# Layer 0's edge sum of a two-layer graph network: runs of equal nodes added up on VectorE ahead of the matmul

## The chip, the cores and the metric

The kernel runs on one core of a Trainium2 chip. The metric is the device time of one execution, in microseconds (us). Engines are named as the profile does: PE is TensorE (PEld its weight loads), DVE VectorE, ACT ScalarE, POOL GpSimd, SP SyncE. A q behind the name is the engine's own sequencer.

## The reference

12,500 nodes with 128 features, 200,000 edges sorted by their destination `dst`, 50 features per edge.

```python
h = relu(layernorm(x))
x = x + (segment_sum(h[src], dst) @ W_rel.T + b_rel + h @ W_root.T)      # layer 0
h = relu(layernorm(x))
edge_weights = silu(edge_attr @ We1 + be1) @ We2 + be2                   # layer 1
agg = segment_sum(h[src] * edge_weights, dst)
x = x + (silu(agg @ Wn1 + bn1) @ Wn2 + bn2)
```

Everything is float32.

## The kernel before

The edges are cut into tiles of 128, four tiles to a block of 512 (`BLOCK`), 391 blocks, and 17 blocks (`U`) to one of 23 iterations (`ITERS`). Three blocks are a group (`GB`): six groups per iteration (`G`), five of 12 tiles and a last one of 8. Since the edges are sorted, those of a group lie within a window of 128 neighbouring nodes, whose first node is `sum_base`.

GpSimd gathers the rows of h by `src`, one indirect DMA per tile, 68 per iteration (L324), into `rows`, which holds one whole iteration. Before it gathers a group it waits (`hold`, L192) for the sum of the same group of the iteration before, `s_seg`; at the first and the fourth group it also waits for the indices, which SyncE loads half an iteration at a time.

For each group VectorE compares an iota with the tiles' `dst` less the window's base and gets a one-hot of 128 x 1536 (L744, `s_onehot`). TensorE multiplies the rows of each of the 12 tiles with its one-hot and accumulates in the bank `seg` or `ew_a` in turn (L377, `s_seg`): the transposed sum of the window. One group later VectorE reads the window's base into a register and adds the bank to `agg` at that place (`add_window`, L752 to L756). `agg` lies as 128 features x 12,800 nodes.

In the same iterations one group of 512 nodes is finished per iteration (`node_update0`): ScalarE copies `agg` and h, TensorE multiplies (L388, L389, at group 1), VectorE adds bias and x and takes the statistics for layer 1's layer norm (group 3), the shift (group 4) and y (group 5).

Before all this there are a setup (windows of all groups, from the block minima and maxima of `dst`) and the h phase, five passes over five groups of 512 nodes each, in which h is computed and written to `h_rows`. GpSimd gathers iteration 0 meanwhile, from x, since h isn't there; iteration 0 therefore applies the layer norm to the gathered rows itself, block by block (L658 to L669). The whole of layer 0 may run over several passes, if a window is wider than 128 nodes; the number is computed on the chip (`plan`), and is one here.

Layer 1 runs in 23 iterations of the same shape, with the edge network of each block and the same one-hots and sums.

Each engine has its own queue of instructions in the order in which it is written out; semaphores alone tie them together. In particular nothing but `s_onehot`, the landed rows and, for GpSimd, `s_seg` orders the three engines in layer 0.

## Time and profile before

| what | us |
|---|---|
| median of 3 runs | 4755.86 (4752.82 to 4757.91) |
| the profiled execution | 4776.76 |
| its span | 4774.7 |
| setup and h phase, to 162 | 162 |
| iteration 0, 162 to 248 | 86 |
| layer 0, 248 to 2293, 21 periods | 2045 |
| end of layer 0, 2293 to 2391 | 98 |
| layer 1, from 2391 | 2383 |

The stages are cut by the timeline, at the first one-hot of VectorE, at its first add of iteration 1, and at the starts of the later iterations. A row of the timeline gives the start, the busy time, the engine, the line and the operation, and in brackets the time for which the engine was idle before it and what ended that. "issue" means that it waited for nothing that the profile shows, "remote" a semaphore whose sender isn't told.

### The profile page before, as it was taken

How to read it: one execution, taken by the hardware profiler on the slowest of the kernel's cores; microseconds unless marked ns; L12 is line 12 of the kernel's file. 1: busy time of each engine (PE TensorE's matmuls, PEld its weight loads, DVE VectorE, ACT ScalarE, POOL GpSimd, SP SyncE). 2: the span in 40 equal slices, each digit the busy share in tenths (PEclk: the TensorE clock that was granted, in tenths of full speed). 3: DMA queues.
4: the chain of work that ended last, by engine and by line, in shares of the span. 5: the costliest groups of instructions: out<-in, count | busy, mean ns of one | idle time of the engine just before them, and what ended most of it. 6: DMA issues, size and time to landing. Idle time of an engine off the chain costs nothing.

```text
span 4774.7 us, 34714 instructions
## 1 busy us (share of the span) xinstructions
PE 2496.3 (52%) x10150; PEld 1646.9 (34%) x10150; DVE 1005.3 (21%) x1790; ACT 704.4 (15%) x1212; POOL 2967.1 (62%) x3135
## 2 busy tenths in 40 slices
PE   1332322323232322233347777777776777777778
PEld 0232322222232322232224444444443444434444
DVE  2511111111111111111312222222222222222223
ACT  2400000000000000000112222222222222212222
POOL 5366666666666666666466666666666666666663
PEclk9765655555555655655668777877777877877878
DMA  4212222212222222212212222222222222222222
GB/s 131 67 52 54 52 55 56 54 51 56 54 56 54 53 54 55 54 51 56 64 53 70 65 63 65 68 65 70 66 66 62 69 65 70 66 63 68 66 65 62
DMA packets 230577, 296.69 MB, mean 62 GB/s; under 512 B 68707, under 2 KB 160277, under 8 KB 230432
## 3 DMA queue, kind: packets, MB, share of 16 engines
q0 software_dynamic: 100096, 205.20, 16.6%
q10 hardware_dynamic: 61378, 60.59, 4.6%
q1 hardware_dynamic: 69086, 30.73, 2.4%
q8 instruction: 5, 0.08, 0.0%
q14 instruction: 12, 0.10, 0.0%
HBM read 269.81 MB, written 26.48 MB: 62 GB/s over the span
## 4 chain that ended last, share of the span: by engine, by line
another core or an unknown queue 44%; PE 28%; issue 17%; DVE 6%; DVEq 2%; ACT 1%; POOL 0%; DMA 0%; ACTq 0%; SPq 0%; POOLq 0%
PE seg L377 10%; PE hid_b L419 3%; PE hid_a L424 3%; DVE onehot L744 3%; PE ew_a L377 2%; PE hid_c L424 2%; PE ew_b L430 2%; PE hid_b L424 2%; PE ew_a L430 1%; DVEq L752 1%; PE hid_a L419 1%; PE hid_c L419 1%; DVE agg L756 1%; DVE e_stats L658 1%
## 5 line engine op out<-in xcount | busy, mean ns | idle before, releaser
L324 POOL DMA_INDIRECT rows<-h_rows,idx x3060 | 2902.0, 948 | 1723.0 <-issue 946.8
L377 PE MATMUL seg<-onehot,rows 128*128 128x128 f32 x4784 | 884.3, 340 | 1347.0 <-DVE onehot L744 523.8
L377 PEld LDWEIGHTS seg<-onehot,rows 128*128 128x128 f32 x4784 | 802.1, 250 | 1460.5 <-issue 1038.9
L377 PE MATMUL ew_a<-onehot,rows 128*128 128x128 f32 x1472 | 289.0, 324 | 574.3 <-issue 529.2
L744 DVE TENSOR_TENSOR onehot<-iota_ps,dst_rel 128x1536 f32<-128x1536 f32 (+1 forms) x278 | 461.0, 1658 | 0.8 <-DVE dst_rel L732 0.6
L377 PEld LDWEIGHTS ew_a<-onehot,rows 128*128 128x128 f32 x1472 | 246.6, 235 | 570.5 <-issue 566.5
L852 DVE TENSOR_TENSOR rows<-ew_a,rows 128x512 f32<-128x512 f32 x207 | 142.8, 690 | 1110.6 <-remote 636.3
L756 DVE TENSOR_TENSOR agg<-seg,agg 128x128 f32 x207 | 60.4, 292 | 1179.3 <-remote 1110.5
L424 PE MATMUL hid_c<-hidden,we_sb 128*128 128x512 f32 x230 | 149.4, 735 | 161.6 <-ACT hidden L601 160.4
L852 DVE TENSOR_TENSOR rows<-ew_b,rows 128x512 f32<-128x512 f32 x184 | 126.7, 689 | 507.2 <-PE ew_b L430 173.2
L424 PE MATMUL hid_a<-hidden,we_sb 128*128 128x512 f32 x278 | 219.6, 882 | 0.0
L424 PE MATMUL hid_b<-hidden,we_sb 128*128 128x512 f32 x276 | 178.8, 734 | 37.4 <-ACT hidden L601 37.4
L756 DVE TENSOR_TENSOR agg<-ew_a,agg 128x128 f32 x69 | 19.8, 288 | 802.4 <-remote 779.0
L430 PEld LDWEIGHTS ew_a<-ident,agg 128*128 128x128 f32 x828 | 127.8, 170 | 159.4 <-issue 157.0
L601 ACT ACTIVATE hidden<-hid_a,be_col 128x512 f32<-128x512 f32 x139 | 95.6, 688 | 521.8 <-remote 401.3
L601 ACT ACTIVATE hidden<-hid_b,be_col 128x512 f32<-128x512 f32 x139 | 95.6, 687 | 474.2 <-PE hid_b L419 195.1
L601 ACT ACTIVATE hidden<-hid_c,be_col 128x512 f32<-128x512 f32 x115 | 79.1, 688 | 578.2 <-remote 419.4
L534 ACT ACTIVATE n_std<-n_mv,eps 128x4 f32<-128x4 f32 x25 | 7.4, 297 | 1022.8 <-issue 702.9
L430 PE MATMUL ew_a<-ident,agg 128*128 128x128 f32 x828 | 156.6, 323 | 2.8 <-issue 2.8
L430 PEld LDWEIGHTS ew_b<-ident,agg 128*128 128x128 f32 x736 | 107.5, 163 | 132.9 <-issue 118.4
L546 ACT ACTIVATE hT<-agg 128x512 f32 x23 | 14.5, 629 | 922.7 <-DMA y_rows<-ys 917.0
L430 PE MATMUL ew_b<-ident,agg 128*128 128x128 f32 x736 | 132.9, 311 | 0.9 <-issue 0.9
(134 smaller groups left out, 1851.1 us busy)
## 6 DMA issues: line engine op xcount, KB each, us to landing
rows<-h_rows,idx POOLq DMA_INDIRECT x3060
ef_a<-ef_blocks ACTq DMA_DIRECT2D x70, 300.0 KB
node_work<-ef_blocks ACTq DMA_DIRECT2D x47, 300.0 KB
xs<-x SPq DMA_DIRECT2D x40, 256.0 KB
ys<-y_rows SPq DMA_DIRECT2D x26, 256.0 KB
out<-xs ACTq DMA_DIRECT2D x26, 256.0 KB
y_rows<-ys ACTq DMA_DIRECT2D x25, 256.0 KB
h_rows<-node_work ACTq DMA_DIRECT2D x23, 256.0 KB
```

Of the source, the lines that this page charges most:

```text
L324: pool.indirect_dma_start(out=rows[:, u, t, :], out_offset=None, in_=table, in_offset=bass.IndirectOffsetOnAxis(ap=idx[:, j:j + 1], axis=0 ...
L377: mm = pe.matmul(seg[layer][g % 2][:, 0:P], rows[:, u, t, :], onehot[:, g % 2, k * TB + t, :], start=(k == 0 and t == 0), stop=(last and t ...
L419: pe.matmul(hid_ps[u % 3][:, :], we1_sb[:, :], ef[g % 2][:, k, :], start=True, stop=True).then_inc(s_hid, 1)
L424: pe.matmul(hid_ps[u % 3][:, :], we2_sb[:, :], hidden[:, u % 2, :], start=True, stop=True).then_inc(s_ew_t, 1)
L430: tr = pe.transpose(ew_ps[u % 2][:, t * P:(t + 1) * P], weights[:, u % 2, t * P:(t + 1) * P], ident[:, :])
L546: nc.scalar.activation(hT[r], h_table[:, bass.ds(g * BLOCK, BLOCK)], ACT.Copy)
L601: nc.scalar.activation(hidden[:, u % 2, :], hid_ps[u % 3][:, :], ACT.Silu, bias=be1_col[:, :]).then_inc(s_silu, 1)
L658: op = v.bn_stats(e_stats[:, u, t, :], src[:, t, :])
L744: return v.tensor_tensor(onehot[:, g % 2, 0:tiles, :], iota_ps[:, 0:P].unsqueeze(1).to_broadcast([P, tiles, P]), dst_rel[:, bass.ds(it * U ...
L752: base = dve.value_load(base_row[0:1, bass.ds(it * G + g, 1)], min_val=0, max_val=BASE_MAX)
L756: v.tensor_tensor(window, seg[layer][g % 2][:, 0:P], window, ALU.add).then_inc(s_acc[layer], 1)
L852: v.tensor_tensor(rows[:, u, :, :], ew, rows[:, u, :, :], ALU.mult).then_inc(s_msg, 1)
```

## The change

On the host the edges of a group are dealt out differently: partition p of a group's tiles holds 12 edges that are neighbours in the sorted order (8 in the last group), where before neighbours lay in neighbouring partitions. Within such a stretch equal nodes stand together, as runs. The kernel numbers the runs of each stretch once, in the setup (`run_of`, a scan over changes of `dst`), and the nodes they belong to (`run_dst`, `run_targets`). For each group VectorE then, for three runs r (`R`), multiplies the rows with the mask of run r (`masks`, made once per iteration) into three neighbouring PSUM banks, `wide`, and reduces over the 12 edges into 128 x 128 (`run_sums`). TensorE multiplies only these three sums with three one-hots (made for three groups at a time, `one_hots`, twice per iteration). Each multiply waits for the reduce before it, and each reduce for the multiply before it, on semaphores that VectorE itself increments, all against one counter register, `done`. The add into `agg` comes two groups later (`LAG`), with its base loaded once per iteration. GpSimd waits in layer 0 for VectorE's third multiply (`s_pick[2]`) instead of TensorE's sum. TensorE's node product stands at group 2 instead of 1. If a stretch held more than three runs, layer 0 would run in further turns (`passes0`). In the setup, all of this and the clearing of `agg` and the computing of the windows stand ahead of the h phase; before, the latter two came behind it. In layer 1 the load of the base uses fewer register instructions.

The core of the diff:

```diff
+R = 3
+LAG = 2
-                    hold(pool, s_seg[layer], i * G + (g + 1))
+                    if layer == 0:
+                        hold(pool, s_pick[R - 1], i * G + (g + 1))
+                    else:
+                        hold(pool, s_seg[1], i * G + (g + 1))
...
+            v.tensor_scalar(dst_flat, dst_flat, 1.0, None, ALU.add)
+            v.memset(scratch, 1.0).then_inc(s_setup, 1)
...
+            v.tensor_tensor_scan(run_of, scratch, run_of, 0.0, ALU.mult, ALU.add).then_inc(s_setup, 1)
...
+            v.memset(agg[0][:, :], 0.0)
...
+            v.tensor_tensor(plan[:, 0:1], plan[:, 2:3], run_wrap[0:1, :], ALU.mult).then_inc(s_plan, 1)
+            run_targets(0)
...
-            v.memset(agg[0][:, :], 0.0)
...
+            def run_sums(g):
+
+                dve.reg_add(done, done, 1)
+                tiles = len(blocks_of(g)) * TB
+                first = g * GB
+                for r in range(R):
+                    dve.wait_ge(s_sum[(r + R - 1) % R], done)
+                    v.tensor_tensor(picked[:, 0:tiles, :],
+                                    rows[:, first:first + tiles // TB, :, :].rearrange("p k t f -> p (k t) f"),
+                                    run_mask[:, r, first * TB:first * TB + tiles].unsqueeze(2)
+                                    .to_broadcast([P, tiles, P]),
+                                    ALU.mult).then_inc(s_pick[r], 1)
+                    dve.wait_ge(s_pick[r], done)
+                    v.tensor_reduce(run_sum[g % SUM_BUFS][:, r, :], picked[:, 0:tiles, :].rearrange("p e f -> p f e"),
+                                    AX.X, ALU.add).then_inc(s_sum[r], 1)
+
+            def add_runs(g, base, value):
+
+                window = agg[0][:, bass.ds(base, P)]
+                dve.wait_ge(s_seg[0], value)
+                v.tensor_tensor(window, run_seg[g % 3][:, 0:P], window, ALU.add).then_inc(s_acc[0], 1)
...
                     for g in range(G):
-                        if g > 0:
-                            add_window(0, i, it, g - 1)
-                        else:
-                            add_window(0, i - 1, it - 1, G - 1)
-                        one_hot(it + (g + 1) // G, (g + 1) % G).then_inc(s_onehot, 1)
+                        if g == 0:
+                            hold(dve, s_mask, i + 1)
+                        dve.wait_ge(s_rows[0][g], landed_full if g < G - 1 else landed_last)
+                        run_sums(g)
+                        add_runs((g + G - LAG) % G, window_at[g], done)
+                        if g == LAG - 1:
+                            one_hots(it, 1)
+                        if g == HALF_G + 1:
+                            one_hots(it + 1, 0)
                         if g in steps:
                             steps[g]()
```

What stands in VectorE's queue in an iteration of layer 0 for one group. Before, the add of the group before and the next one-hot:

```order
L752 ISA
L752 TENSOR_LOAD base_row
L752 ISA x2
L754 REGISTER_ALU
L755 REGISTER_ALU [waits s_acc_done0]
L756 ISA [waits s_seg_done0]
L756 TENSOR_TENSOR agg<-seg,agg 128x128
L744 ISA
L744 TENSOR_TENSOR onehot<-iota_ps,dst_rel 128x1536
```

Now, the group with index 2 (the sums of groups lie in turn in three places, two of them in `onehot`'s memory, one in `hidden`'s):

```order
L876 REGISTER_ALU [waits s_rows0_2]
L881 TENSOR_TENSOR wide<-rows,consts_ps 128x1536 [waits s_sum2]
L887 TENSOR_REDUCE hidden<-wide 128x128 [waits s_pick0]
L881 TENSOR_TENSOR wide<-rows,consts_ps 128x1536 [waits s_sum0]
L887 TENSOR_REDUCE hidden<-wide 128x128 [waits s_pick1]
L881 TENSOR_TENSOR wide<-rows,consts_ps 128x1536 [waits s_sum1]
L887 TENSOR_REDUCE hidden<-wide 128x128 [waits s_pick2]
L894 ISA [waits s_seg_done0]
L894 TENSOR_TENSOR agg<-seg,agg 128x128
```

One long instruction per group became six, each with a wait for the one ahead of it, and the load of the base is gone.

TensorE's queue at the same place, before, with the node product behind group 0:

```order
L399 ISA
L406 ISA [waits s_onehot]
L377 MATMUL seg<-onehot,rows 128x128 [waits s_rows0_0]
L377 MATMUL seg<-onehot,rows 128x128 x11
L385 ISA
L388 MATMUL node<-w_root_sb,hT 128x128 [waits s_nT]
L389 MATMUL node<-w_rel_sb,node_work 128x128
```

and now, groups 0 and 1 and then the node product:

```order
L406 MATMUL seg<-onehot 128x128 [waits s_sum2]
L406 MATMUL seg<-onehot 128x128 x2
L404 REGISTER_ALU
L406 MATMUL ew_a<-onehot 128x128 [waits s_sum2]
L406 MATMUL ew_a<-onehot 128x128 x2
L424 ISA
L427 MATMUL node<-w_root_sb,hT 128x128 [waits s_nT]
L428 MATMUL node<-w_rel_sb,node_work 128x128
```

Twelve matmuls became three, both of whose operands VectorE writes, and the product moved one group back.

## Rows read from the trace of the kernel before

**Rows 1.** The costliest group of instructions; busy us, mean ns, idle before it:

```profile
L324 POOL DMA_INDIRECT rows<-h_rows,idx x3060 | 2902.0, 948 | 1723.0 <-issue 946.8
```

**Rows 2.** Busy time by stage; columns as in the first line:

```profile
core 0: us, PE busy (x) PEld busy (x) DVE busy (x) ACT busy (x) POOL busy (x), PEclk, DMA share, GB/s
162.00:248.00 86.00, 34.20 (x138) 29.72 (x139) 37.04 (x182) 31.82 (x86) 47.64 (x51) 0.60 0.16 41
248.00:2293.00 2045.00, 612.45 (x3192) 544.12 (x3191) 304.44 (x524) 64.42 (x146) 1347.37 (x1427) 0.59 0.21 54
```

**Rows 3.** POOL's idle time before gathers, 248 to 2293; us, times:

```profile
  issue: 422.0, 1385
  remote: 275.9, 42
```

**Rows 4.** POOL's timeline: first gathers after a pause, layer 0, last row layer 1:

```profile
1024.84 0.94 POOL L324 DMA_INDIRECT rows<-h_rows,idx  x1 [6.81 <-remote]
...
1070.86 0.94 POOL L324 DMA_INDIRECT rows<-h_rows,idx  x1 [6.36 <-remote]
...
1122.30 0.94 POOL L324 DMA_INDIRECT rows<-h_rows,idx  x1 [6.77 <-remote]
...
3023.13 0.94 POOL L324 DMA_INDIRECT rows<-h_rows,idx  x1 [3.18 <-remote]
```

**Rows 5.** PE's timeline, before and after the restart at 1070.86:

```profile
1062.25 0.37 PE L377 MATMUL seg<-onehot,rows 128*128 128x128 f32 x1 [2.43 <-issue]
...
1076.03 2.84 PE L377 MATMUL seg<-onehot,rows 128*128 128x128 f32 x24
```

**Rows 6.** Busy time in three stretches, layer 0 and layer 1:

```profile
1024.80:1036.00 11.20, 8.50 (x57) 8.31 (x58) 5.84 (x6) 1.15 (x2) 8.50 (x9) 0.78 0.36 95
1036.00:1068.50 32.50, 6.00 (x17) 4.29 (x16) 0.00 (x0) 0.00 (x0) 21.71 (x23) 0.56 0.19 49
...
3005.20:3020.00 14.80, 13.59 (x48) 7.67 (x47) 3.16 (x4) 3.49 (x6) 11.33 (x12) 0.77 0.23 63
```

**Rows 7.** DVE's timeline in the h phase, under gathers:

```profile
24.71 0.38 DVE L662 BATCH_NORM_AGGREGATE e_mv<-e_stats 128x2 f32<-128x6 f32 x4 [5.47 <-remote]
25.01 0.14 DVE L667 RECIPROCAL e_rstd<-e_std 128x4 f32<-128x4 f32 x1
31.64 0.16 DVE L669 SCALAR_TENSOR_TENSOR e_shift<-e_mv,e_rstd 128x4 f32<-128x4 f32 x1 [6.49 <-remote]
```

**Rows 8.** DVE's timeline in layer 0, outside the stretched time:

```profile
1073.23 1.75 DVE L744 TENSOR_TENSOR onehot<-iota_ps,dst_rel 128x1536 f32<-128x1536 f32 x1
1074.90 0.69 DVE L788 TENSOR_TENSOR node<-node,b_rel_all 128x512 f32<-128x512 f32 x1
1075.71 0.69 DVE L792 TENSOR_TENSOR xs<-node,xs 128x512 f32<-128x512 f32 x1
...
1081.17 1.22 DVE L744 TENSOR_TENSOR onehot<-iota_ps,dst_rel 128x1024 f32<-128x1024 f32 x1
```

**Rows 9.** DVE's timeline in setup, h phase and iteration 0:

```profile
9.08 2.28 DVE L655 TENSOR_REDUCE hi_sb<-agg 128x4 int32<-128x2048 int32 x1
...
115.48 0.69 DVE L679 COPY agg<-hid_c 128x512 f32 x1 [0.19 <-PE hid_c L364]
...
128.12 0.69 DVE L679 COPY agg<-hid_c 128x512 f32 x1 [0.20 <-PE hid_c L364]
...
144.04 10.72 DVE L689 MEMSET agg<- 128x12800 f32 x1 [2.62 <-issue]
...
159.29 1.59 DVE L728 TENSOR_TENSOR dst_rel<-dst_sb,sum_base 128x1380 f32<-128x1380 int32 x1 [1.63 <-issue]
...
168.19 0.18 DVE L667 RECIPROCAL e_rstd<-e_std 128x4 f32<-128x4 f32 x1 [0.64 <-ACT e_std L523]
```

**Rows 10.** Busy time in one iteration of layer 0:

```profile
1024.80:1122.30 97.50, 29.46 (x152) 25.84 (x152) 14.59 (x26) 3.09 (x7) 64.22 (x68) 0.59 0.21 54
```

**Rows 11.** DVE's timeline at the end of layer 0:

```profile
2291.63 0.29 DVE L756 TENSOR_TENSOR agg<-seg,agg 128x128 f32 x1 [40.44 <-remote]
...
2335.30 0.28 DVE L756 TENSOR_TENSOR agg<-ew_a,agg 128x128 f32 x1
```

More of the change, by code:

```diff
@@ L278, in next_idx @@
                 load_idx(it + 1, HALF, U, s_idx_b)
-            with sp.Fori(0, passes) as p:
+            with sp.Fori(0, passes0) as p:
                 next_idx(0, p * ITERS, 0)
@@ L356, in _ @@
             pe.wait_ge(s_ident, 1)
+            pe.wait_ge(s_run, 1)
+            pe.matmul(node[:, 0:P], scratch[:, 0:P], ident[:, :], start=True, stop=True).then_inc(s_run_max, 1)
             with pe.Fori(0, GROUPS // H_SETS) as k:
@@ L451, in _ @@
             edge_weights(0, 0)
-            with pe.Fori(0, passes) as p:
+            with pe.Fori(0, passes1) as p:
                 with pe.Fori(0, ITERS) as it:
@@ L563, in node_update0 @@
                 return {0: turned, 1: lambda: node_std(n, r), 2: h1, 3: y, 4: stored}
[L565 removed]
+            with act.Fori(0, passes0) as p:
                 edge_std(p * U, 0)
@@ L611, in _ @@
             edge_silu(0, 0)
-            with act.Fori(0, passes) as p:
+            with act.Fori(0, passes1) as p:
                 with act.Fori(0, ITERS) as it:
@@ L639, in _ @@
             v = nc.vector
+            for r in range(R):
+                dve.sem_inc(s_pick[r], G)
+                dve.sem_inc(s_sum[r], G + (r == R - 1))
+            dve.sem_inc(s_seg[0], G + LAG)
+            done = dve.alloc_register("sums_done")
+            dve.reg_mov(done, G)
             dve.sem_inc(s_acc[0], 1)
@@ new lines, in _ @@
+            dve.wait_ge(s_setup, 13)
+            v.tensor_scalar(plan[:, 2:3], plan[:, 2:3], 1.0, None, ALU.add)
+            v.tensor_scalar(span[:, 1:2], span[:, 1:2], 0.0, 1.0 - LATE_STEPS, ALU.is_ge, ALU.mult).then_inc(s_setup, 1)
+            dve.wait_ge(s_setup, 14)
+            v.tensor_scalar(plan[:, 1:2], span[:, 1:2], float(LATE_STEPS), None, ALU.add)
+            dve.wait_ge(s_run_max, 1)
+            v.tensor_reduce(run_last[:, :], node[:, 0:P], AX.X, ALU.max).then_inc(s_setup, 1)
@@ L806, in _ @@
                 hold(dve, s_hcopy[r], GROUPS // H_SETS + 1)
-            with dve.Fori(0, passes) as p:
-                one_hot(0, 0).then_inc(s_onehot, 1)
+            with dve.Fori(0, passes0) as p:
+                masks(0)
+                one_hots(0, 0)
+                one_hots(0, 1)
                 edge_stats(p, 0)
@@ L878, in edge_blocks @@
                         steps[u]()
-            with dve.Fori(0, passes) as p:
+            with dve.Fori(0, passes1) as p:
                 one_hot(0, 0)
```

319 lines of the change are left out of this document (215 added, 104 removed).

## The prediction

> **What bounds the kernel now.** I read the page first: the costliest group are GpSimd's (POOL's) 3060 gathers of 948 ns, 2902 us [rows 1]. Then the table by stage: after 162 us of setup and h phase 86 us of iteration 0, 2045 us for the 21 periods after it in layer 0 [rows 2]; what follows is layer 0's end and layer 1, which the change hardly touches. In the 2045 us GpSimd is busy for 1347 us, and it idles 422 us in 1385 short issue gaps (0.30 us each) and 276 us in 42 pauses that a semaphore ends: two per iteration, 6.6 us each [rows 3]. So an iteration is 68 gathers of 0.945 + 0.30 us, 84.9 us, and two pauses, together 97.5 us, as the restarts at 1024.84 and 1122.30 say [rows 4]. Layer 0 would not be faster than 84.9 us an iteration, whatever the other engines did. What can be won is 12.6 us, 21 times: 264 us.
>
> Why does GpSimd pause at all? A group is gathered again when its sum of the iteration before is there, so GpSimd has a whole iteration of slack and still catches up. TensorE's own rows tell why [rows 5]: 24 matmuls took 2.84 us at 1076.03, but at 1062.25 a single one of 0.37 us starts 2.43 us after the one before, "by issue", so it waits for no data. All engines share that state. The cycle's windows show it: in the 11.2 us after GpSimd resumes, 132 instructions are recorded (57 + 58 + 6 + 2 + 9); in the next 32.5 us TensorE has 17 matmuls and 16 loads and VectorE none [rows 6]. It ends in GpSimd's pause, which here began at 1064.50 (1070.86 less 6.36, [rows 4]). I call it stretched. The traces show that it comes with unbroken gathering, not with a wait in the program.
>
> VectorE under gathers in the h phase gives the price: between 24.71 and 31.64 it completed five instructions (four aggregates and one reciprocal), 1.39 us each, where they last 0.1 us [rows 7]. An instruction that waits for the one before it waits for the whole queue: idle for 5.47 and 6.49 us there. Outside that state a wait for its own last result costs 0.12 us (1074.90 + 0.69 to 1075.71) [rows 8].
>
> **The change, part by part.** (1) *VectorE, natural price.* I price every new operation over 1536 elements as the one-hot, 1.75 us, with 0.12 us for its own wait; over 1024 as the short one, 1.22 [rows 8]. Multiply from SBUF and reduce from PSUM are not in layer 0 of this trace; the integer reduction over 2048 elements (2.28 us, [rows 9]) gives 1.71 us for 1536. Five full groups have 6 such operations each, 5 x 6 x 1.87 = 56.1; the last 6 x 1.34 = 8.0; six adds at 0.29 [rows 11] are 1.7; masks (204 elements) and two one-hots (1152) 2.9; the node steps 4.6 (13 instructions of the kernel before, of which two stand in [rows 8]). That is 73.3 us per iteration, against 84.9 of gathering: 12.2 us per group, hidden as long as VectorE isn't stretched. Before, VectorE was busy 304 us in the whole stage [rows 2], so this engine becomes the second longest.
>
> (2) *VectorE, stretched.* At 1.4 us per completed instruction a 1.75 us operation with its own wait behind it takes two slots, 2.8: 30 x 2.8 = 84, the last group's six one slot each, 8.4, adds 8.4, masks and one-hots 4.9, 13 node instructions 18.2. Sum 124 us per iteration. Bounds of the self-wait: 0.12 us below, 5 to 6.5 above, where a queue of four or five lies ahead of it. Here each instruction waits for its predecessor, so one at most lies ahead, and I take the two slots.
>
> (3) *TensorE.* 68 matmuls of an iteration become 18. Recorded: 152 + 152 now, with the loads [rows 10]; 32 of those 304 are the node product's, and a matmul is four records, so 18 x 4 + 32 = 104 remain. GpSimd now waits for VectorE's last product and not for TensorE's sum; the sum has two groups, 24 us or more, until the add wants it. This wait goes, for 0 us of cost; if TensorE is stretched, six loads and six matmuls of a group take 12 x 1.4 = 17 us, still inside. The node product moves one group later and its reader stands at group 3, one group behind it: 32 records at 1.4 are 45 us in the worst place, a bound I leave to the range.
>
> (4) *How much of the time is stretched.* I take it to follow from gathering and instruction load together: 132 instructions filled it in 11.2 us, while layer 1, with 117 in the 14.8 us between two pauses of 3.2 us [rows 4, 6], isn't stretched. After, an iteration has 58 on VectorE, 104 on TensorE, 7 on ScalarE and 68 on GpSimd, 237 in 84.9 us, 2.8 per us; the same 132 then take 47 us. In 47 clear us VectorE gains 47/73.3 - 47/84.9 = 0.088 iteration on GpSimd, in a pause of 6.5 us 0.089; stretched it loses 1/84.9 - 1/124 = 0.0037 per us, so 47.5 us pass until GpSimd must pause. One cycle is 47 + 47.5 + 6.5 = 101 us with 94.5 of gathering, and an iteration 84.9 x 101/94.5 = 90.7, say 91. 21 x (91 - 97.5) = **-137 us**. Bounds: 84.9 (never stretched) is -264; stretched from 11.2 us on is 98.6 us by the same working (gain 0.021 + 0.089, 29.4 us, cycle 47), +23; with a self-wait of 5.1 us besides, 6.85 x 36 + 30 = 277 us stretched, it is 107.5, +210.
>
> The Trainium skill, page "NOTIFIC — the notification-queue block", section "7.1 Overflow: three behaviours, one of which stalls the engine", says that the block's internal queues always push back on the producers of records and never lose one. By it the stretch would be a matter of how many instructions are recorded, which fits the load above; no row here shows that queue.
>
> (5) *Setup.* About ten passes over 1564 or 1380 elements, 1.59 us for 1380 [rows 9], and small ones, some 20 us, and the memset (10.72) with the windows (2.8) moved ahead of the h loop. All that lies beside the gathers of iteration 0, where the h loop crept anyway: three of its five passes take 12.64 us each (115.48 to 128.12, [rows 9]) and lie behind the gathers, two took all the time before, to 103. I let it begin near 76 and do most of its work clear, 92 to 155; memset and windows no longer follow. First work of iteration 0 at 158 instead of 161.8: **-4** (-15 to +25: the new part has some 60 instructions, 84 us at 1.4).
>
> (6) *Iteration 0.* 17 blocks of layer norm take 2.3 us each when clear, 0.64 of it idle for ScalarE [rows 9], which sums now can fill: 28 to 39 us. With 64 us of sums and 3 of masks and one-hots it is 95 to 106 clear, say 100. The 86 us of before [rows 2] hold 39 of layer norm and 10 of one-hots; the rest, 37, is stretching and waits. Its gathers start group by group behind VectorE, so pauses are frequent and I give it less than half, 15: 115, **+29** (+12 to +64).
>
> (7) *End of layer 0.* The last iteration starts when GpSimd has its last release (2291.63) and TensorE works its backlog off at some 3 us a group [rows 5]: the last add is at 2335.30, 43.7 us later [rows 11]. VectorE with a full iteration behind it needs 73.3 + 8 + 1.7 = 83: **+39**; 0 if it isn't behind.
>
> (8) *Layer 1.* Code as before, but one base load with fewer register instructions. It is bound by its gathers and its pauses; 0, and -10 to +10.
>
> Sum: -4 + 29 + 39 - 137 = -73 us. The profiled execution was 4776.76 with a span of 4774.7, 20.9 above the median of 4755.86; the sum is a difference and I lay it on the median: **4683 us**, 1.5% less.
>
> **Rivals.** *Relief*: with 40% fewer instructions the state never forms in layer 0. For it: layer 1's streaks; against: the h phase, stretched with few TensorE instructions at all. Iterations 85.5, 21 x -12 = -252; iteration 0 +15; the end 0. 4755.86 - 4 + 15 - 252 = 4515.
>
> *VectorE's chain becomes the bound*, the slower side: the state comes with gathering alone, 11 us after each restart, and each operation pays for its predecessor. An iteration is 98.6 us or more, pauses shorter and more frequent: -4 + 29 + 39 + 23 = +87, 4843; with longer self-waits up to 5030. It decides from 94.5 us per iteration (64 us of one-time cost over 21). For it: VectorE's idle times of 5.47 and 6.49 us before an instruction that waits for its own last result [rows 7]; against: those had four or five instructions queued ahead.
>
> *It sums twice*: if a partition's stretch held over three nodes, layer 0 would run a second time, +2000 us. From the inputs drawn as the reference draws them, at most three occur in its 17,664 stretches (150 times). 0.01.
>
> **How the numbers follow.** Within 0.2% (about what a measurement can tell here, 9.5 us) lies only a thin slice of iteration times around 94.5. Forecast (88 to 94): 0.36; relief: 0.22; the chain: 0.33; same: 0.08; twice: 0.01. Faster 0.58, same 0.08, slower 0.34. The range reaches from relief with its lower iteration-0 cost, 4500, to the chain with half of its longer waits, 4880.
>
> **What would show it.** Right: GpSimd's wait pauses in the steady stage near one per iteration; restarts 91 us apart; runs of VectorE's multiply and reduce 1.87 us apart for some 40 us and 2.8 apart for as long; the last add some 80 us after the last release. Relief: no pauses over 1 us. Chain: pauses after every one or two groups, operations 2.8 us or more apart most of the time. A reduce or multiply that lasts over 2.3 us (12.2 to 14.2 us per group) would make VectorE the bound without any stretching, and the forecast wrong.

## The result and the profile after

The changed kernel is slower: 4852.94 us (4838.43 to 4870.38, 4 runs) against 4754.34 us (4748.51 to 4757.91), a ratio of 1.022 with a 95% interval of 1.0197 to 1.0243. Two later measurements beside other kernels gave 1.018 (1.0128 to 1.0235) and 1.0183 (1.0151 to 1.0216).

The engines in the page of the kernel before, and then the page of the kernel after, its engines and its costliest groups; beside [rows 1], GpSimd's gathers take what they took, and VectorE's share has gone from 21% to 47%:

```profile
PE 2496.3 (52%) x10150; PEld 1646.9 (34%) x10150; DVE 1005.3 (21%) x1790; ACT 704.4 (15%) x1212; POOL 2967.1 (62%) x3135
```

```profile
span 4847.2 us, 29925 instructions
PE 2119.2 (44%) x7852; PEld 1307.5 (27%) x7852; DVE 2255.7 (47%) x2592; ACT 705.1 (15%) x1212; POOL 2972.2 (61%) x3135
...
L355 POOL DMA_INDIRECT rows<-h_rows,idx x3060 | 2900.4, 948 | 1788.8 <-issue 1039.0
L881 DVE TENSOR_TENSOR wide<-rows,consts_ps 128x1536 f32<-128x1536 f32 (+1 forms) x414 | 691.5, 1670 | 33.2 <-issue 21.1
...
L887 DVE TENSOR_REDUCE onehot<-wide 128x128 f32<-128x1536 f32 x276 | 484.9, 1757 | 9.7 <-DVE wide L881 0.2
```

Where the time went is read from events at the same places of VectorE's queue in both timelines; they are not the same instructions, since those changed. VectorE's timeline after: its first work of iteration 0, of iteration 1 and of the last iteration (the masks), and the last add:

```profile
148.90 0.38 DVE L861 TENSOR_TENSOR consts_ps<-dst_rel,consts_ps 128x204 f32<-128x204 f32 x1 [1.58 <-ACT agg L545]
...
251.18 0.36 DVE L861 TENSOR_TENSOR consts_ps<-dst_rel,consts_ps 128x204 f32<-128x204 f32 x1
...
2341.61 0.37 DVE L861 TENSOR_TENSOR consts_ps<-dst_rel,consts_ps 128x204 f32<-128x204 f32 x1
...
2414.87 0.29 DVE L894 TENSOR_TENSOR agg<-ew_b,agg 128x128 f32 x1 [0.72 <-PE ew_b L406]
```

The corresponding points of the kernel before, in its VectorE timeline, with the first one-hot, the first add of iteration 1 and that of the last iteration; its last add is in [rows 11]:

```profile
161.77 1.76 DVE L744 TENSOR_TENSOR onehot<-iota_ps,dst_rel 128x1536 f32<-128x1536 f32 x1 [0.63 <-DVE dst_rel L732]
...
248.05 0.29 DVE L756 TENSOR_TENSOR agg<-ew_a,agg 128x128 f32 x1 [1.66 <-PE ew_a L377]
...
2294.16 0.28 DVE L756 TENSOR_TENSOR agg<-ew_a,agg 128x128 f32 x1
```

| part | before | after | difference | forecast |
|---|---|---|---|---|
| to the start of iteration 0 | 161.8 | 148.9 | -12.9 | -4 |
| iteration 0 | 86.3 | 102.3 | +16.0 | +29 |
| 21 periods | 2046.1 | 2090.4 | +44.3 | -137 |
| the last iteration | 41.1 | 73.3 | +32.1 | +39 |
| to layer 1's first gather | 27.7 | 33.5 | +5.8 | 0 |
| layer 1 | 2411.7 | 2398.8 | -12.9 | 0 |

That is the difference of the two traces' spans, 72.5 us. The medians differ by 98.6 us: the traced execution of the kernel before lay 22.4 us above its median and that of the changed kernel 3.9 below, and what this is made of isn't in the table. `before_2` and `after_2`, which ran on one chip, have spans 71.0 us apart. One period lasted 99.5 us where it had been 97.4 and where 91 was forecast.

The rows below are GpSimd's waits before its gathers from 251 to 2342 us, to be laid beside [rows 3]. The total that is named is the same 276 us, in 27 waits instead of 42. But the profile marks some of the new pauses with "issue", the longest of them 9.6 us. Counted over all gaps above 2 us, it is 298 us in 23 pauses, 13 us each, against 276 in 42. Ten of the other gaps are longer than before as well (0.5 to 1.2 us instead of 0.30):

```profile
  issue: 459.6, 1410
  DVE wide L881: 276.1, 27
```

What VectorE waited for in the same time (engine, line, what ended the wait, us in total, times, longest; two smaller rows, 13.2 us before L894, are left out):

```profile
DVE node L943 <- remote: 270.9, 13, 29.7
DVE agg L894 <- remote: 155.4, 29, 8.1
DVE node L943 <- issue: 96.0, 7, 20.9
DVE agg L894 <- issue: 90.2, 16, 8.1
DVE wide L881 <- issue: 19.1, 21, 2.0
```

L943 is the first of the node steps, which reads the product; L894 is the add into `agg`. There is no line for L887, and L881 stands with 19 us in 21 waits: the multiplies and reduces that wait for each other lose next to nothing. Together the two readers of TensorE's results wait 626 us, 30 us per period; with VectorE's own work of 68.8 us (`a_quarter_gathers_2`, below) and the 0.9 before L881 it is the period of 99.5.

One such wait in the timelines, VectorE and then TensorE:

```profile
1095.72 0.28 DVE L894 TENSOR_TENSOR agg<-ew_a,agg 128x128 f32 x1
1116.49 0.70 DVE L943 TENSOR_TENSOR node<-node,b_rel_all 128x512 f32<-128x512 f32 x1 [20.49 <-remote]
```

```profile
1077.20 0.39 PE L428 MATMUL node<-w_rel_sb,node_work 128*128 128x128 f32 x2
...
1085.02 1.65 PE L406 MATMUL ew_b<-onehot,hidden 128*128 128x128 f32 x6 [7.44 <-DVE hidden L887]
```

The product was complete at 1077.59. VectorE, which needed it from 1096.00 on, went on at 1116.49, 38.9 us after the end that the profile gives for the work. TensorE itself was not held up; it computed the next group meanwhile. I call this time a **late completion**. It is no fixed time: over the 21 periods, L943 started 19 to 58 us after the product's end. The kernel before has it too: the sum of one group was complete at 1045.77 and its add ran at 1070.23, 24.5 us later. There TensorE's own matmuls are stretched besides [rows 5].

Adds of three groups in a row, whose matmuls had ended long before:

```profile
1263.39 0.29 DVE L894 TENSOR_TENSOR agg<-ew_b,agg 128x128 f32 x1 [4.47 <-remote]
...
1280.19 0.29 DVE L894 TENSOR_TENSOR agg<-seg,agg 128x128 f32 x1 [4.61 <-issue]
...
1296.99 0.29 DVE L894 TENSOR_TENSOR agg<-ew_a,agg 128x128 f32 x1 [5.87 <-issue]
```

They stand 16.8 us apart. A group's three matmuls are 12 instructions of TensorE in the profile, so that is 1.4 us for each.

### The profile page after: what moved, and what is told of

Read it like the earlier page. It is cut to its first block, busy times and chain, and to the rows that moved or that the text cites. A ratio compares the mean times of both kernels' runs of the same rounds, so it can differ in the third digit from the quotient of the medians.

```text
span 4847.2 us, 29925 instructions
## 1 busy us (share of the span) xinstructions
PE 2119.2 (44%) x7852; PEld 1307.5 (27%) x7852; DVE 2255.7 (47%) x2592; ACT 705.1 (15%) x1212; POOL 2972.2 (61%) x3135
## 4 chain that ended last, share of the span: by engine, by line
DVE 30%; another core or an unknown queue 29%; PE 23%; issue 14%; ACT 2%; DVEq 1%; POOL 0%; DMA 0%; ACTq 0%; SPq 0%; POOLq 0%
DVE wide L881 13%; DVE onehot L887 7%; PE wide L457 7%; PE wide L452 6%; PE seg L416 6%; DVE hidden L887 3%; PE ew_b L463 2%; PE ew_a L463 1%; DVE onehot L870 1%; DVEq L898 1%; DVE agg L894 1%; DVE onehot L852 0%; DVE n_stats L924 0%; DVE agg L911 0%
## 5 line engine op out<-in xcount | busy, mean ns | idle before, releaser
L881 DVE TENSOR_TENSOR wide<-rows,consts_ps 128x1536 f32<-128x1536 f32 (+1 forms) x414 | 691.5, 1670 | 33.2 <-issue 21.1
L416 PE MATMUL seg<-onehot,rows 128*128 128x128 f32 x3128 | 531.1, 325 | 372.7 <-DVE agg L911 300.8
L457 PE MATMUL wide<-hidden,we_sb 128*128 128x512 f32 x784 | 547.4, 787 | 222.1 <-ACT hidden L634 210.4
L416 PEld LDWEIGHTS seg<-onehot,rows 128*128 128x128 f32 x3128 | 487.8, 237 | 406.3 <-DVE agg L911 321.4
L634 ACT ACTIVATE hidden<-wide,be_col 128x512 f32<-128x512 f32 x393 | 270.2, 688 | 1599.4 <-remote 935.4
L887 DVE TENSOR_REDUCE onehot<-wide 128x128 f32<-128x1536 f32 x276 | 484.9, 1757 | 9.7 <-DVE wide L881 0.2
L639 ACT ACTIVATE agg<-wide,be_col 128x512 f32<-128x512 f32 x392 | 268.6, 685 | 249.1 <-PE wide L457 121.4
L452 PE MATMUL wide<-ef_a,we_sb 50*128 50x512 f32 x418 | 270.4, 731 | 29.0 <-DMA ef_a<-ef_blocks 28.2
L452 PE MATMUL wide<-node_work,we_sb 50*128 50x512 f32 x368 | 272.7, 829 | 0.0
L852 DVE TENSOR_TENSOR onehot<-consts_ps,dst_rel 128x1536 f32<-128x1536 f32 x139 | 230.6, 1659 | 0.2 <-DVE base_row L1015 0.2
L887 DVE TENSOR_REDUCE hidden<-wide 128x128 f32<-128x1536 f32 (+1 forms) x138 | 205.7, 1490 | 4.8
L943 DVE TENSOR_TENSOR node<-node,b_rel_all 128x512 f32<-128x512 f32 x23 | 16.1, 698 | 367.4 <-remote 270.9
```

The lines of the kernel that those rows point to most:

```text
L416: mm = pe.matmul(seg_ps[:, 0:P], rows[:, u, t, :], onehot[:, g % 2, k * TB + t, :], start=(k == 0 and t == 0), stop=(last and t == TB - 1))
L452: pe.matmul(hid_ps[u % 3][:, :], we1_sb[:, :], ef[g % 2][:, k, :], start=True, stop=True).then_inc(s_hid, 1)
L457: pe.matmul(hid_ps[u % 3][:, :], we2_sb[:, :], hidden[:, u % 2, :], start=True, stop=True).then_inc(s_ew_t, 1)
L634: nc.scalar.activation(hidden[:, u % 2, :], hid_ps[u % 3][:, :], ACT.Silu, bias=be1_col[:, :]).then_inc(s_silu, 1)
L639: nc.scalar.activation(weights[:, u % 2, :], hid_ps[u % 3][:, :], ACT.Identity, bias=be2_col[:, :]).then_inc(s_weights, 1)
L852: return v.tensor_tensor(onehot[:, g % 2, 0:tiles, :], iota_ps.unsqueeze(1).to_broadcast([P, tiles, P]), dst_rel[:, bass.ds(it * U + g * G ...
```

## Experiments

Two theories stood against each other. **Late completions**: while GpSimd gathers without a break, the end of each TensorE instruction (matmul and weight load apart, four to a float32 matmul) is seen about 1.4 us after that of the one before, in order; a reader waits for all that are ahead. **Chain**: VectorE's six dependent operations per group are the bound. Each kernel is compared with the kernel before on the same chip. A number of instructions of TensorE ("records") per iteration of layer 0 is counted from the code: 4 x 18 + 32 = 104 in the changed kernel.

### TensorE's work made smaller, VectorE's chain left alone

`a_short_product`, in TensorE's node product:

```diff
-                    for t in range(TB):
-                        o = node_o[r][:, t * D:(t + 1) * D]
-                        pe.matmul(o, hT[r][:, t * P:(t + 1) * P], w_root_sb[:, :], start=True, stop=False)
-                        mm = pe.matmul(o, aggT[r][:, t * P:(t + 1) * P], w_rel_sb[:, :], start=False, stop=True)
+                    mm = pe.matmul(node_o[r][:, :], hT[r][:, 0:P], aggT[r][:, :], start=True, stop=True)
```

> The changed kernel with the eight matmuls of the node product in layer 0 replaced by one of 128x512, so that the product leaves 4 records instead of 32 (the node values are not the reference's). Completions theory: while GpSimd gathers, each TensorE record takes 1.4 us until its semaphore is seen, and VectorE at L943 waits for the product's (367 us of idle in 25 waits). Then these waits fall below 60 us, restarts come every 87 to 91 us instead of 99.6, and the time is 4600 to 4690. Chain theory (VectorE's six dependent operations per group are the bound): nothing changes, 4830 to 4870.

Measured: 4749.95 us against 4748.26, ratio 1.0005 (0.9975 to 1.0035). The waits at the product's reader fell from 367 to some 85 us, and the restarts 982.53 and 1458.78, five iterations apart, give 95.3 us for one. So 103 us were won back, and VectorE's chain is not the bound; but 4690, and the 60 us of waits, were missed, because the mean of these periods came no lower than 95.3, and the end of layer 0 stayed as long. The eight executions had granted clocks from 0.671 to 0.885 and times from 4724 to 4767 us without an order between the two, so TensorE's clock is not what decides.

`a_one_matmul`:

```diff
-                for r in range(R):
+                for r in (R - 1,):
                     mm = pe.matmul(run_seg[g % 3][:, 0:P], run_sum[g % SUM_BUFS][:, r, :], run_hot[g][:, r, :],
-                                   start=(r == 0), stop=(r == R - 1))
+                                   start=True, stop=True)
```

> The changed kernel with one of the three matmuls per group in layer 0 (the sums of runs 0 and 1 are left out of the result), 4 records per group instead of 12. Completions theory: 12 records x 1.4 = 16.8 us per group is what the adds wait for (262 us of idle before L894); those waits fall below 60 us, those for the product stay, iterations 90 to 95, time 4660 to 4760. Chain theory: VectorE's work is the same, 4830 to 4870.

Measured: 4682.07 us, ratio 0.9859 (0.9818 to 0.9900), in the range of the completions theory, though the waits for the product, which were to stay, fell to 29 us in five, the last at 614 us. Its trace holds what neither theory had said. GpSimd's gathers from 700 to 2240 us (count, shortest, median and longest ns; idle before them; who waited for them) and VectorE's waits in the same time:

```profile
L355 POOL DMA_INDIRECT rows<-h_rows,idx x1100: 940/1092/1935, 699.8 to 2238.9; - x184
...
  issue: 358.8, 1100
...
  DVE wide L881: 424.1, 81
```

```profile
DVE wide L881 <- DMA rows<-h_rows,idx: 424.1, 81, 7.7
```

No pause at all, and VectorE waits for nothing but gathered rows: GpSimd is the bound, as the forecast's relief had it. But 1100 gathers took 1540 us, 1.40 each, since the gather itself now takes 1.09 us and not 0.945:

```profile
1001.26 1.09 POOL L355 DMA_INDIRECT rows<-h_rows,idx  x1 [0.30 <-issue]
1002.66 1.10 POOL L355 DMA_INDIRECT rows<-h_rows,idx  x1 [0.30 <-issue]
1004.06 1.09 POOL L355 DMA_INDIRECT rows<-h_rows,idx  x1 [0.31 <-issue]
```

68 x 1.40 is 95.2 us. That, and not 84.9, is what the iterations settle at here; only the gathers of iterations 2 and 3 still took 85.2 us each. Of the 97.4 us of before 2.2 were to be had, and 3.3 on the mean of the 21 periods.

The same trace limits the completions theory. The product's last matmul ended at 1244.21, GpSimd gathered without a pause, and VectorE read the product at 1273.24 without waiting: its 32 records were seen within 29 us, under 0.91 us each. So 1.4 us per record is no constant of unbroken gathering; what sets it stays open.

`a_steps_late`, on VectorE:

```diff
-                    steps = node_update0(n, 0, n + 1)
+                    update = node_update0(n, 0, n + 1)
+                    steps = {5: lambda: [update[k]() for k in (3, 4, 5)]}
```

> The changed kernel with VectorE's three node steps (x1, shift, y) all behind group 5 instead of behind groups 3, 4 and 5; nothing left out. Completions theory: the product's semaphore has two groups more, 24 us or more, so the wait at L943 falls from 16 us per iteration to about 2, against some 4 us of waits for ScalarE's steps; iterations near 92, time 4670 to 4740. Chain theory: the same operations in the same queue, 4830 to 4870.

Measured: 4934.2 us, ratio 1.039 (1.0331 to 1.0449). A clear miss, and a useful one. The wait for the product vanished, and this took its place, where the adds had waited 259 us before:

```profile
DVE agg L894 <- remote: 527.3, 46, 40.9
```

As I read it, the sums of the next groups stand behind the product's 32 records on TensorE, so their completions are as late as the product's; an add that follows two groups behind can't do without them. A wait that is moved past a late completion meets the next one.

`b_quarter`, the kernel before with one tile of four in layer 0's sums:

```diff
-                for t in range(TB):
+                tiles = range(TB) if layer == 1 else (TB - 1,)
+                for t in tiles:
...
-                                   start=(k == 0 and t == 0), stop=(last and t == TB - 1))
+                                   start=(k == 0 and t == tiles[0]), stop=(last and t == TB - 1))
```

> The kernel before with one matmul per block instead of four in layer 0 (three of four tiles are left out of the sum): 12 records per group as in the changed kernel, but no chain on VectorE and the product's reader two groups behind it. Completions theory: GpSimd's pauses of 6.6 us fall to under 2, iterations 85 to 88, time 4540 to 4610. If the pauses come from gathering alone, whatever TensorE has to do, the time stays near 4755.

Measured: 4714.39 us, ratio 0.9928 (0.9901 to 0.9955). Faster, as forecast, but by 34 us where some 140 to 210 were expected. TensorE's 304 records per iteration became 100 (17 matmuls of four, and the product's 32), and the period fell by 1.7 us only: it is mostly the pace of the gathers, and not the number of records, that holds the kernel before at 97.4. GpSimd now gathers 136 tiles, two iterations, and then pauses:

```profile
481.96 0.94 POOL L324 DMA_INDIRECT rows<-h_rows,idx  x1 [21.24 <-remote]
...
673.28 0.94 POOL L324 DMA_INDIRECT rows<-h_rows,idx  x1 [21.37 <-remote]
```

191.3 us for two, 95.7 each: with pauses of 21 us at 1.25 us per gather, or without any at 1.40, the mean stays nearly the same.

### Another chip

The next three kernels ran on a chip on which the kernel before takes 3999.52 us instead of about 4750.

> The changed kernel in which, from iteration 1 of layer 0 on, only one of the four tiles of each block is gathered (the other rows keep the values of iteration 0, so layer 0's sums are wrong). Nothing is changed on VectorE, TensorE or ScalarE. If the delay of semaphores belongs to gathering, iterations last what VectorE's own work lasts, 72 to 76 us, the waits before L943 vanish (under 20 us in all) and the time is 4180 to 4300. If TensorE's semaphores come late whatever GpSimd does, the waits stay at 16 us per iteration and the time stays above 4600.

> The changed kernel with each multiply and reduce over 4 of a group's tiles instead of 12 or 8 (the rest is left out of the sums): 0.7 us instead of 1.75 per operation, same number of instructions, same waits. Completions theory (TensorE's 104 records per iteration at 1.4 us are what is waited for): iterations 95 to 98, and only the end of layer 0 gets shorter, by 30 to 45 us; time 4700 to 4780; under gathers VectorE's operations stand 1.4 us apart though they last 0.7. Chain theory (VectorE's work of 73 us per iteration is the bound): the iteration falls to gathering alone and the time to 4560 to 4620.

> The changed kernel with a third of the rows, one run instead of three and one matmul per group, and the node product as one matmul: TensorE has 28 records per iteration and VectorE some 34 (sums and node values aren't the reference's). If 1.40 us per gather (95.2 us per iteration), seen in the kernel with one matmul per group, is what unbroken gathering itself can keep up, this one has the same iterations, 94 to 95.5, and takes 4660 to 4700. If it came from what TensorE and VectorE did beside it, gathers keep 1.25 us, iterations are 85 and the time is 4460 to 4500.

Measured: 3751.72 us (0.9378, interval 0.9351 to 0.9406), 4032.91 (1.009, 1.0067 to 1.0113) and 4021.39 (1.0053, 1.0030 to 1.0076). GpSimd's gathers in `a_light` there:

```profile
L355 POOL DMA_INDIRECT rows<-h_rows,idx x1494: 940/944/1081, 132.4 to 1995.9; - x187
...
  issue: 455.3, 1494
```

22 iterations of unbroken gathering at 1.25 us, and no wait of VectorE for TensorE in any of the three from 250 us to the end of the steady stage. These three could not tell the theories apart. What they say is another thing: where completions aren't late, an iteration is 84.9 to 85.3 us wherever all rows are gathered, and only iteration 0 and the end of layer 0 are left. Each version with more work on VectorE and all gathers lost 22 to 52 us there. A name that ends in _2 or _3 is the same kernel again, on a chip of the first sort.

### VectorE's chain made smaller, and the bare gathers

On a chip with 4803.52 us for the kernel before, beside the changed kernel and the kernel before as they are.

> The changed kernel as it is. On a chip on which the kernel before takes about 4000 us (there gathers keep 1.25 us unbroken and no semaphore comes late), both have iterations of 84.9 us, and only iteration 0 (+5 to +15) and VectorE's longer last group (+10 to +20) remain: 4015 to 4045, ratio 1.004 to 1.011. On a chip on which it takes 4750: again 4840 to 4870.

> The kernel before as it is, for its trace beside the others of this call. If the chip is one on which it takes about 4000 us: no pause of GpSimd over 1 us in layer 0's iterations and 84.9 us between them; layer 1 in 1980 to 1990 us instead of 2400. Else as the first trace: two pauses of 6.6 us per iteration, 97.5 us.

`after_2` took 4896.35 us (ratio 1.0181) and `before_2` 4799.07 (0.9986, 0.9968 to 1.0005); its pauses were 6.3 and 6.8 us as in [rows 4].

`a_third_chain_2` multiplies and reduces over 4 tiles only:

```diff
+                blocks = tiles // TB
+                tiles = TB
...
-                                    rows[:, first:first + tiles // TB, :, :].rearrange("p k t f -> p (k t) f"),
+                                    rows[:, first + blocks - 1:first + blocks, :, :].rearrange("p k t f -> p (k t) f"),
```

> The kernel a_third_chain (multiply and reduce over 4 tiles, the rest left out of the sums). On a chip with late semaphores (before at 4750): completions theory, iterations 95 to 98 and 4700 to 4780, VectorE's short operations 1.4 us apart; chain theory, 4560 to 4620. On one without: as before, ratio 1.009.

Measured: 4839.82 us, ratio 1.0071 (1.0048 to 1.0095), 57 us less than `after_2`. In the two traces the last iteration is 21 us shorter, iteration 0 5 and the 21 periods together 23, so the chain costs a little there, but it isn't the bound of the period. Its operations take 0.69 us instead of 1.76, some 35 us less per iteration, and two iterations still take 198.5 us, 99.3 each, as in the changed kernel:

```profile
2027.17 0.95 POOL L355 DMA_INDIRECT rows<-h_rows,idx  x1 [24.92 <-DVE wide L883]
...
2225.68 0.94 POOL L355 DMA_INDIRECT rows<-h_rows,idx  x1 [25.49 <-DVE wide L883]
```

VectorE waits in the two readers instead, for the product and for the sums:

```profile
DVE node L945 <- remote: 565.4, 18, 42.3
DVE agg L896 <- remote: 556.8, 51, 12.3
```

The chain theory is out. The number in my expectation for the completions theory was missed as well (4700 to 4780, 95 to 98 us): the layout with the reader one group behind the product costs more than I gave it. That its operations would stand 1.4 us apart was not seen either; they stood 0.73 apart wherever they ran, here 24 us into an unbroken streak of gathers:

```profile
1059.30 0.69 DVE L889 TENSOR_REDUCE onehot<-wide 128x128 f32<-128x512 f32 x1
1060.03 0.69 DVE L883 TENSOR_TENSOR wide<-rows,consts_ps 128x512 f32<-128x512 f32 x1
```

`a_light_2` leaves a third of the rows, one run and one matmul per group and the short product, 28 records on TensorE.

> The kernel a_light (a third of the rows, one run, one matmul per group, the product as one matmul; results left out accordingly). On a chip with late semaphores: 95.2 us per iteration and 4660 to 4700 if 1.40 us per gather is gathering's own sustained rate there; 85 and 4460 to 4500 if it came from the other engines. On one without: ratio 1.005 again.

Measured: 4722.78 us, ratio 0.9830 (0.9769 to 0.9891); the iterations are those forecast for gathering's own pace, the time is 23 us above the range. Gathers from 700 to 2240 us:

```profile
L355 POOL DMA_INDIRECT rows<-h_rows,idx x1097: 942/947/2636, 699.2 to 2239.2; - x183
```

1097 in 1540 us, 1.40 each, with little beside them. The pace belongs to the gathers on this sort of chip, not to the load of the other engines.

### The number of records up and down, and the gathers

`a_bf16`, `a_double_matmul` and `a_quarter_gathers_2` ran on one chip, the kernel before at 4790.53 us. The first writes run sums and one-hots as bfloat16, whose matmul leaves two records instead of four; the core of the edit:

```diff
+        BF16 = mybir.dt.bfloat16
+        run_hot = [x.bitcast(BF16)[:, :, 0:P] for x in run_hot]
+        run_hots = [x.bitcast(BF16)[:, :, 0:P] for x in run_hots]
+        run_sum = [x.bitcast(BF16)[:, :, 0:P] for x in run_sum]
```

> The changed kernel with the run sums and their one-hots written in bfloat16, so that each of the 18 sum matmuls of an iteration leaves 2 records instead of 4: 36 + 32 = 68 per iteration instead of 104 (run sums are rounded to bfloat16). Where the kernel before takes 4750 to 4800 us: completions theory, 68 x 1.4 = 95.2 fits just into an iteration of gathering, so the waits before L894 go and those for the product shrink; iterations 95 to 97, VectorE less behind at the end, ratio 0.975 to 0.99. Chain theory: as the changed kernel, 1.018 to 1.022.

> The changed kernel with each of the three sum matmuls of a group issued a second time into an unused part of the bank: 24 records per group, 176 per iteration instead of 104; the result is untouched and TensorE has idle time enough, its matmuls take 1.6 us per group. Completions theory: 24 x 1.4 = 33.6 us per group under gathering; the adds wait longer, iterations 106 to 125, ratio 1.05 to 1.15. Chain theory: nothing changes, 1.018 to 1.022.

> The kernel a_quarter_gathers (one of four tiles of each block gathered from iteration 1 on), on a chip on which the kernel before takes 4750 to 4800. If late semaphores belong to gathering: iterations of 68.8 us as on the other chip, no wait over 1 us at L943, layer 0 shorter by 21 x 28 us or more, time 4200 to 4320 (ratio 0.88 to 0.91). If they come with the chip whatever GpSimd does: iterations over 90.

The second adds three matmuls whose result nobody reads:

```diff
                 for r in range(R):
+                    pe.matmul(run_seg[g % 3][:, P:2 * P], run_sum[g % SUM_BUFS][:, r, :], run_hot[g][:, r, :],
+                              start=True, stop=True)
+                for r in range(R):
```

and the third leaves out three of four gathers (the counts of landed rows that others wait for are lowered to match, which isn't shown):

```diff
+                            if few and t:
+                                continue
                             pool.indirect_dma_start(
```

`a_bf16`: 4749.81 us, 0.9926 (0.9906 to 0.9946), 0.7% faster than the kernel before, but short of the 0.975 to 0.99 that was forecast. `a_double_matmul`: 5035.52 us, 1.0527 (1.0481 to 1.0572). `a_quarter_gathers_2`: 4216.77 us, 0.8815 (0.8776 to 0.8854). One period in each, from GpSimd's restarts in the first two and from VectorE's masks in the third:

```profile
792.62 0.94 POOL L359 DMA_INDIRECT rows<-h_rows,idx  x1 [4.27 <-DVE wide L885]
...
887.90 0.94 POOL L359 DMA_INDIRECT rows<-h_rows,idx  x1 [4.28 <-DVE wide L885]
```

```profile
999.68 0.94 POOL L355 DMA_INDIRECT rows<-h_rows,idx  x1 [23.30 <-DVE wide L884]
...
1107.48 0.94 POOL L355 DMA_INDIRECT rows<-h_rows,idx  x1 [23.23 <-DVE wide L884]
```

```profile
1009.14 0.37 DVE L868 TENSOR_TENSOR consts_ps<-dst_rel,consts_ps 128x204 f32<-128x204 f32 x1
1077.94 0.37 DVE L868 TENSOR_TENSOR consts_ps<-dst_rel,consts_ps 128x204 f32<-128x204 f32 x1
```

95.3, 107.8 and 68.8 us. Work that TensorE does in its idle time, and that nobody waits for, costs 8 us per iteration. Its own duration is no likely cause: three matmuls more are some 1.6 us per group, and the add has two groups of time. That leaves its completions. Without three quarters of the gathers no reader waits for TensorE in the steady stage (the product was read 18 to 19 us after its end, without a wait), and the period is VectorE's own work, 68.8 us. So the lateness belongs to gathering, its price rises with the number of TensorE's instructions, and the chain would have been hidden behind 95.2 us.

In `a_bf16` the waits before the adds are gone, but the product's reader waits 26.4 us in each iteration, 531 us in all, where less than the changed kernel's 367 was forecast. It starts 44.8 us after the product's end (1733.03 and 1688.25), which is 32 x 1.4, and it costs the period nothing. It leaves VectorE an iteration behind at the end; I took that for the last thing to be had, with `a_steps_late`'s edit on top of `a_bf16`.

> The kernel a_bf16 (run sums and their one-hots in bfloat16) with VectorE's three node steps behind group 5, as in a_steps_late. In a_bf16 an iteration lasts 95.3 us, which is what gathering alone took, but VectorE waits 26.5 us in each for the product and so ends layer 0 a whole iteration behind GpSimd: 90 us from its last gather to layer 1's first. If that wait is what holds it back, it falls under 5 us here, iterations stay at 95 to 96, and the gap before layer 1 falls from 90 to 50 or 60 us: ratio to the kernel before 0.980 to 0.987, against 0.9926 of a_bf16. If TensorE's records were still too many for late steps, as in a_steps_late (1.039), it is above a_bf16.

On the other sort of chip it took 4052.62 us against 4000.76, ratio 1.013 (1.0113 to 1.0147). `a_bf16_late_2` is the same kernel on the first sort, with the changed kernel beside it.

> The kernel a_bf16_late again, since its first run fell on a chip on which the kernel before takes 4000 us. Where it takes 4750 to 4800: product wait under 5 us per iteration, 95 to 96 us per iteration, gap before layer 1 50 to 60 us instead of 90, ratio 0.980 to 0.987; above 0.9926 if the later reader doesn't help.

> The changed kernel as it is, beside it. Where the kernel before takes 4750 to 4800: 1.018 to 1.022, as in the two measurements so far. Where it takes 4000: iterations of 84.9 us as in the kernel before, more only in iteration 0 and at the end of layer 0, ratio 1.007 to 1.015.

`a_bf16_late_2`: 4765.99 us, ratio 0.9936 (0.9912 to 0.9959), no better than `a_bf16`; from the last gather of layer 0 to the first of layer 1 it took 94 us, not 50 to 60. VectorE waits for an add again, once per iteration, behind the product's 32 records:

```profile
DVE agg L900 <- remote: 427.2, 19, 23.2
```

`after_3`: 4882.08 us, 1.0183.

Periods of layer 0 on the chips with late completions, by TensorE's records. They are from the steady stretch, except for the changed kernel and the kernel before, whose period is the mean of 21:

| kernel | records | period us |
|---|---|---|
| a_light_2 | 28 | 95.5 |
| a_one_matmul | 56 | 95.2 |
| a_bf16 | 68 | 95.3 |
| a_short_product | 76 | 95.3 |
| b_quarter (product's reader two groups behind) | 100 | 95.7 |
| the changed kernel | 104 | 99.5 |
| a_third_chain_2 | 104 | 99.3 |
| a_steps_late | 104 | 103.4 |
| a_double_matmul | 176 | 107.8 |
| the kernel before | 304 | 97.4 |

The last row doesn't fit a rule by number alone. What differs is that the kernel before lets three groups of TensorE run off within 12 us of a restart, where each group of the changed kernel first needs its 10.8 us on VectorE; `a_third_chain_2`, in which that is 4.3 us, was no faster, so this alone doesn't explain it, and why 304 records cost less there than 176 here stays open. A test of the product's place alone was not made.

## Why the prediction was wrong

**The direction** failed: 1.5% faster was forecast, 2.2% slower was measured. The time lies in the range, near the 4843 us of the rival *VectorE's chain becomes the bound*, but not by its mechanism. That rival's period (98.6) was nearly met by coincidence.

**Step (4)**, -137 us against +44.3, is the one that turned the sign. Three things in it were wrong. First, its lower bound and the sentence "Layer 0 would not be faster than 84.9 us an iteration": the 84.9 us are right as a bound but can't be reached here, since gathers that don't pause slow down to 1.40 us each, 95.2 us. The trace of before could only show streaks of 32 and 36 gathers between pauses and one of 68, all at 1.25. So 12.6 us per iteration were held to be there, and 2.2 to 3.3 were. The best case, *relief*, was the larger error: it would have been 4682 at best and not 4515, as `a_one_matmul` shows.

Second, where the lateness bites. I gave it to VectorE, from its own slow rows in the h phase [rows 7], and let TensorE's results be hidden behind two groups. It was the other way round. VectorE's waits for itself cost 0.03 to 0.04 us throughout (1058.48 + 1.76 to 1060.28), while TensorE completes 32 in 3 us and its readers wait. It is tempting to say that VectorE is spared because one instruction in 1.79 us is slower than one per 1.4, but `a_third_chain_2` speaks against it: there its instructions followed each other every 0.73 us under gathers, and none was held up. So the prediction's "All engines share that state" did not hold for VectorE in layer 0, and why its waits in the h phase are long [rows 7] and these are not stays open.

Third, step (3) said of the product that moves one group later: "32 records at 1.4 are 45 us in the worst place, a bound I leave to the range". It is a common case and not the worst, which was 58 us. The wait was 367 us in 21 periods (20 waits), the largest wait of the stage, and should have been a term of the sum and a rival. The adds' waits, 259 us, follow from 12 records x 1.4 = 16.8 us per group, which step (3) had as 17 and called inside. It is inside for one group, but not when each follows the other, for 16.8 is more than the 15 us of a group's gathers.

**Step (1)** was good: 73.3 us of VectorE per iteration were forecast, 68.8 it was (`a_quarter_gathers_2`). The multiply and the reduce take 1.76 us, where 1.75 was taken from the one-hot. Waits for itself were even cheaper than 0.12.

**Step (2)**, the 2.8 us slots, was wrong: nothing in the trace after shows them, and with them falls the 124 us per iteration on which step (4)'s cycle of 101 us rests.

**Step (5)**, setup: -12.9 us, within its range, -4 forecast. The new part ran at full speed, from 11.4 to 52.9 us, and VectorE's first long wait came only at 61 us (3.44 us, before 64.35), where it had come at 15 (2.85 us, before 18.30). **Step (6)**: +16.0 against +29; iteration 0 ran without stretching, so my 15 us for it were not needed. **Step (7)**: +32.1 against +39, and right in its reason: VectorE is a full iteration behind. 5.8 us more pass until layer 1's first gather, of which I had nothing.

**Layer 1**: 12.9 us less in this pair of traces, outside the -10 to +10 of step (8), and 18.5 less in the pair from one chip, `before_2` and `after_2` (2435.1 and 2416.6). But `a_third_chain_2` and `a_light_2`, which have the changed kernel's layer 1, took 2428.0 and 2423.9 there, and `b_quarter`, which has that of the kernel before, 2392 elsewhere. Whether the change shortens layer 1 is open.

The Trainium skill, page "NOTIFIC — the notification-queue block", section "7.1 Overflow: three behaviours, one of which stalls the engine", says that the block's internal queues push back on the producers of records and don't lose one. That would agree with `a_double_matmul`, where work without a reader delays what follows it (107.8 us for 99.5). That this block is the cause is argued, not shown: every execution here with a span and a granted clock was recorded, and no run shows whether completions are late without the recording.

## What to carry to other kernels

A semaphore can arrive long after the work is done: put the end of the producer's last instruction beside the start of the waiter, and if tens of us lie between with the producer idle or at other work, count the producer's instructions and not its busy time. Make a burst smaller before you move its reader: fewer instructions won 103 us (`a_short_product`), while a later reader cost 1.7% more (`a_steps_late`, 1.039 for 1.022), since what the producer did after the burst was late as well. And don't take the pace of an engine between two pauses for the pace that it would keep without them; a test with the rest taken away gives that number in one run.

## What was not expected of the hardware

- **Late completions.** While GpSimd gathers unbroken, the waiters for TensorE go on late: 38.9 us after a product of 32 records, 16.8 us per group of 12. With a quarter of the gathers no one waits. With 56 records per iteration instead of 104 (`a_one_matmul`) no one waited after 614 us either, under gathers that never paused.
- **Gathers have two paces.** On the chips where the kernel before takes 4750 us or more, 1.25 us each in streaks of up to 136, 1.40 when they never pause (1100 in 1540 us), with much beside them or little.
- **Chips differ.** The kernel before took 4748 to 4804 us on four chips and 4000 on two others. On the latter 1494 gathers went at 1.25 us without a break, and VectorE did not wait for TensorE in the steady stage. Of the kernels that ran there, none with the run sums was faster than the kernel before, unless it left gathers out; the changed kernel itself was not among them.
- VectorE's reduce of 12 elements at a stride from PSUM takes 1.76 us for 1536 elements, as long as the multiply.
